# Attention inside a transformer block: products in blocks of two key tiles, reciprocals spread differently, the normalising product moved to GpSimd

## The chip, the cores and the metric

One core of a Trainium2 chip runs the whole program in one launch. The metric is device time in microseconds (us). The engines are TensorE (PE in the profile; its weight loads are PEld), VectorE (DVE), ScalarE (ACT), GpSimd (POOL) and SyncE (SP), whose queue issues the transfers.

## The reference

```python
def attn(x, qkv_w, qkv_b, proj_w, proj_b):     # 4 x 2048 tokens, 512 wide, 16 heads of 32
    q, k, v = split(x @ qkv_w.T + qkv_b)
    a = softmax(q @ k.T * 32 ** -0.5)          # per batch and head: 2048 x 2048
    return (a @ v) @ proj_w.T + proj_b
def ffn(x, Wr, br, W1, b1, W2, b2):            # 8 experts; each batch takes its top two by token 0
    h = gelu(x @ W1[idx] + b1[idx])
    return sum(h @ W2[idx] + b2[idx]) / 2
xn = layernorm(x)
out = x + attn(xn, ...) + ffn(xn, ...)
```

Everything is float32.

## The kernel before

There are three stages, one after the other. A dense stage makes queries, keys, values and the expert part; the attention stage (`attention_stage`, line 576) computes the softmax products; an output stage (`output_stage`, line 999) applies the last projection. Only the attention stage is changed.

**Groups and steps.** Four heads are handled together. A group is four heads by 512 queries; there are 64 groups (`NQ * QC`), in turns of `G = 8`, the first and last turn written out and six in a loop between them. Within a group the 2048 keys are 16 tiles of 128 (`KT`), and these are worked off in eight steps j = 0 to 7 (`NP`), two key tiles each.

**What TensorE does.** Its order is written out by hand in `STEPS`, one string a step, one letter a piece of work:

- S, a score product (`scores`, line 951): 128 keys by 512 queries of one head, into one of three banks `st_ps`. ScalarE takes the exponential of it into `p_sb` (line 814). A bank is used again when its exponential is done. 64 a group.
- U, a unit (`unit`, line 890): 128 queries by 512 keys of one head of a *coming* group, into one of three banks `mx_ps`. VectorE takes the largest value of each row (line 829); they become the shift of that group's softmax. Unit n waits until VectorE has reduced unit n - 3. 64 a group.
- V, the products of one key tile (`values`, line 902): four matmuls, one a head, 32 columns of the array each, over 512 queries. They need the key tile's four exponentials.
- Z, sum parts (`sums`, line 910): the same form with ones, over pairs of `p_sb` that GpSimd has added up (lines 756 and 766). `PARTS` says how many parts a Z holds: one in j = 0, 1, 4 and 6, two in j = 7.
- T, the transposition of the row maxima (line 895), once a group, in j = 6; it needs `max_done` of VectorE, and ScalarE makes the shift of it (line 780).

Before the change a step has two V, so a group has 16 places where TensorE goes from U and S to column-wise products and back, four pairs of U and S apart in the main.

**What the other engines do.** After the last product and the last sum part of a group, ScalarE copies `o_ps` to `o_raw` (`copy_o`, line 786, before its fourth exponential of the next group) and `sum_ps` to `sum_raw` (`copy_sum`, line 792). VectorE takes the reciprocals in eight pieces of 64 columns (`invert`, line 843), two in each of j = 2 to 5, and multiplies `o_raw` by them at the start of j = 6 (`normalise`, line 849). SyncE then stores `o_inv` (`store_group`, line 696), queued behind the load of the next shift and ahead of the next queries. GpSimd's order is `ADDS`, ten additions a group of 128 x 2048; the last one, of pair 7, has index 9 and waits for the group's last exponential.

```python
SB = 3
ADDS = [(0, 0, -1), (1, 1, -3), ("four", 1, None), (2, 0, None), (3, 2, -2), ("four", 2, None),
        (4, 0, None), (5, 1, 0), (6, 2, 1), (7, 0, 2)]
```

Of the kernel before, what the change touches and what calls it, by code (L numbers as in the profile page):

```python
# [18 lines left out]
ALU = mybir.AluOpType  # L19
# [14 lines left out]
NQ = B * HQ  # L34
KT = N // P
# [540 lines left out]
def attention_stage(nc, qh_d, ql_d, kh_d, kl_d, v_d, o_d):  # L576
# [6 lines left out]
    QC = N // TOK  # L583
    UN = 4 * TT * (N // 512)
    NP = KT // 2
    INV = 8
    SLOTS = 8
    AHEAD = 6
# [7 lines left out]
    PARTS = [(3, 1, 4), (6, 2, 6), (7, 0, 7), (8, 1, 7), (9, 2, 8), (10, 0, 9)]  # L596
    PAIR_ADDED = [[pair for pair, _, _ in ADDS].index(i) + 1 for i in range(NP)]
    NA, NS = len(ADDS), len(PARTS)
    ctx = ExitStack()
    with ctx:  # L600
        def sb(name, shape, dt):
# [2 lines left out]
        def sem(name):  # L604
# [12 lines left out]
        o_raw = sb("o_raw", [P, TOK], F32)  # L617
        sum_raw = sb("sum_raw", [P, TOK], F32)
        o_inv = sb("o_inv", [P, TOK], F32)
# [13 lines left out]
        exp_done, o_copied, sum_copied, shift_done = sem("exp_done"), sem("o_copied"), sem("sum_copied"), sem("shift_done")  # L633
# [3 lines left out]
        G = 2 * QC  # L637
# [4 lines left out]

        STEPS = ["USUSUSVZUSUSUSUSVUS", "USUSUSVZUSUSUSUSVUS", "USUSUSVUSUSUSUSVUS", "USUSUSVUSUSUSUSVUS",
                 "USUSUSVZUUSUSUSUSVUS", "USUSUSVUUSUSUSUSVUS", "SSSVZTSUSUSUSUVSUU", "USUSUSVZUSUSUSUSVUS"]
        FIRST = sum(s.count("U") for s in STEPS[AHEAD:])

        def unit_at(j, i):
# [7 lines left out]
        def bank(g, m):  # L657
            return (g * SK + m) % SB

        def bank_read(g, m):  # L660

            if m >= SB or g > 0:
                return g * SK + m - SB + 1
            return [n for n in range(-SB, 0) if bank(G, n) == bank(0, m)][0] + 1

        assert units_of(AHEAD - 1)[-1] == UN - 1 and "".join(STEPS).count("U") == UN
        assert all(step.count("S") == 8 for step in STEPS)

        with nc.Block() as block:
# [66 lines left out]
            @block.gpsimd  # L736
            def _(pool):
                pool.memset(ident[:, :], 0.0).then_inc(zeroed, 1)
                pool.wait_ge(zeroed, 1)
                pool.affine_select(out=ident[:, :], in_=ident[:, :], compare_op=ALU.not_equal, fill=1.0, base=0,  # L740
                                   pattern=[[-1, P]], channel_multiplier=1).then_inc(ident_ok, 1)

                pool.wait_ge(ident_ok, 1)
                pool.memset(ones[:, :], 1.0).then_inc(ones_ok, 1)
                for i in range(2):
                    pool.wait_ge(ones_ok, i + 1)
                    pool.memset(k_x[i][R:R + 1, :, :].bitcast(F32), 1.0).then_inc(ones_ok, 1)
                pool.wait_ge(ones_ok, 3)

                def turn(L):  # L750
                    for g in range(G):
                        for n, (i, slot, part) in enumerate(ADDS):
                            done = L * G * NA + g * NA + n
                            if i == "four":
                                pool.wait_ge(pair_done, done)
                                pool.tensor_tensor(p_pair[:, slot, :, :], p_pair[:, 0, :, :], p_pair[:, slot, :, :],  # L756
                                                   ALU.add).then_inc(pair_done, 1)
                                continue

                            pool.wait_ge(exp_done, L * G * SK + g * SK + 8 * i + 8)  # L760
                            if part is None:
                                pool.wait_ge(pair_done, done)
                            else:

                                pool.wait_ge(sum_done, since(L * G * NS, g * NS + part + 1))
                            pool.tensor_tensor(p_pair[:, slot, :, :], p_sb[:, 2 * i % SLOTS, :, :], p_sb[:, (2 * i + 1) % SLOTS, :, :],  # L766
                                               ALU.add).then_inc(pair_done, 1)

                turn(0)
                with pool.Fori(1, TURNS) as L:  # L770
                    turn(L)

            @block.scalar
            def _(act):
# [49 lines left out]
            @block.vector  # L824
            def _(dve):
                def unit(base, n):

                    dve.wait_ge(unit_ready, base + n + 1)
                    dve.reduce_max(unit_max[:, n // 4, n % 4:n % 4 + 1], mx_ps[n % 3][:, :], AX.X).then_inc(unit_done, 1)  # L829

                def rows(base, count):

                    dve.wait_ge(unit_done, base + UN)
                    dve.wait_ge(rows_ready, count - 1)
                    dve.reduce_max(row_max[:, :], unit_max[:, :, :], AX.X).then_inc(max_done, 1)

                def invert(count, part):

                    cols = slice(part * TOK // INV, (part + 1) * TOK // INV)
                    if part == 0:  # L840
                        dve.wait_ge(sum_copied, count)
                        dve.wait_ge(o_st, (count - 1) * 16)
                    dve.reciprocal(o_inv[:, cols], sum_raw[:, cols]).then_inc(inv_done, 1)  # L843

                def normalise(count):

                    dve.wait_ge(inv_done, count * INV)
                    dve.wait_ge(o_copied, count)
                    dve.tensor_tensor(o_inv[:, :], o_raw[:, :], o_inv[:, :], ALU.mult).then_inc(o_done, 1)

                for n in range(UN):
                    unit(0, n)
                rows(0, 1)
                for n in range(FIRST):
                    if n == 0:
                        dve.wait_ge(max_done, 1)
                    unit(UN, n)

                def turn(L, first, last):
                    for g in range(G):  # L860
                        for j in range(NP):
                            ahead = 2 if j >= AHEAD else 1
                            if j == AHEAD and not (first and g == 0):
                                normalise(L * G + g)
                            for i, n in enumerate(units_of(j)):
                                if not (last and g + ahead >= G):
                                    if n == 0:
                                        dve.wait_ge(max_done, L * G + g + 2)
                                    unit((L * G + g + ahead) * UN, n)
                                if 2 <= j < 6 and i in (2, 6) and not (first and g == 0):  # L870
                                    invert(L * G + g, 2 * (j - 2) + (i == 6))
                            if j == AHEAD - 1 and not (last and g + ahead >= G):
                                rows((L * G + g + ahead) * UN, L * G + g + 2)

                turn(0, True, False)
                with dve.Fori(1, TURNS - 1) as L:
                    turn(L, False, False)
                turn(TURNS - 1, False, True)
                for part in range(INV):
                    invert(NQ * QC, part)  # L880
                normalise(NQ * QC)

            @block.tensor
            def _(pe):
# [41 lines left out]
                def turn(L, first, last):  # L926
                    for g in range(G):
# [23 lines left out]
                            pe.matmul(st_ps[bank(g, m)][:, :], k_x[u][:, h, kt * P:(kt + 1) * P], q_x[qc][:, h, :],  # L951
                                      start=True, stop=True).then_inc(st_ready, 1)

                        def products(kt):

                            if kt < 0:
                                if not (first and g == 0):
                                    values(L, (g - 1) * KT + KT - 1, (g - 1) % G // QC, KT - 1)
                                return
                            if kt == 0:  # L960
                                pe.wait_ge(v_ld[u], (L + 1) * 16)
                                if not (first and g == 0):
                                    pe.wait_ge(o_copied, L * G + g)
                            values(L, g * KT + kt, u, kt)

                        def sum_parts(j):

# [8 lines left out]
                        for j in range(NP):  # L976
                            for i, step in enumerate(STEPS[j]):
                                if step == "U":
                                    next_unit(j, unit_at(j, i))
                                elif step == "S":  # L980
                                    scores(8 * j + STEPS[j][:i].count("S"))
                                elif step == "V":
                                    products(2 * j - 1 + STEPS[j][:i].count("V"))
                                elif step == "Z":
                                    sum_parts(j)
                                elif not (last and g == G - 1):
                                    turn_rows(L * G + g + 2)
# [2 lines left out]
                with pe.Fori(1, TURNS - 1) as L:  # L990
                    turn(L, False, False)
                turn(TURNS - 1, False, True)
                values(TURNS - 1, G * KT - 1, 1, KT - 1)
                for i in range(NS):
                    if PARTS[i][2] >= NP:
                        sums(TURNS - 1, G - 1, i)
# [181 lines left out]
```

## Time and profile before

| | |
|---|---|
| time, median of 3 runs | 5173.42 us (5172.55 to 5173.84) |
| the profiled execution's own time | 5168.91 us |
| its span in the trace | 5167.1 us |
| busy: PE, PEld | 97%, 56% of the span |
| busy: DVE, ACT, POOL | 66%, 50%, 63% of the span |
| attention stage | from about 1371 to 4975 us |

Busy shares are means over the three stages. In the timeline view, a row merges neighbouring instructions of one kind: the first number is the start, the second the length in us, x the count, and the bracket the idle time before it with what ended it. Matmuls are pipelined, so a row's length runs into the next row, and it is the distance from start to start that tells what a matmul costs.

### The profile page before, as it was taken

The numbers are of one execution on the slowest core, as the hardware profiler recorded it, in microseconds if no ns is written. First come the engines' busy times: TensorE is split into PE (matmuls) and PEld (weight loads), VectorE is DVE, ScalarE is ACT, GpSimd is POOL, SyncE is SP. The second block draws the span as 40 slices with busy tenths as digits, with TensorE's granted clock in tenths as the row PEclk, the third lists the DMA queues.
The fourth block names the chain that finished last, engine by engine and source line by source line (L and its number), as shares of the span: only waits on it lengthen the run. The fifth ranks groups of instructions, "written<-read, shape, count | busy, mean of one in ns | idle before, by whom it ended". The sixth has DMA issues, their size and how long they took to land. (4 is left out here: it accounts for less than half of the span.)

```text
span 5167.1 us, 83198 instructions
## 1 busy us (share of the span) xinstructions
PE 5031.4 (97%) x25932; PEld 2893.7 (56%) x25932; DVE 3420.5 (66%) x5616; ACT 2592.6 (50%) x4717; POOL 3231.8 (63%) x861
## 2 busy tenths in 40 slices
PE   8999999999899999999999999999999999999979
PEld 6878878788444444444444444444444444444447
DVE  4232232322678888877887887888788788888724
ACT  2121121211266666666666666666666666666631
POOL 1212111121488888887887888788788788888830
PEclk9999999999799999999999999999999999999989
DMA  5253343533402021121202102120220202020046
GB/s 171 88 158 95 117 130 97 153 94 106 102 20 53 17 52 42 32 53 24 50 19 56 48 22 53 24 50 20 57 50 20 56 18 50 20 56 17 7 164 238
DMA packets 186069, 348.49 MB, mean 67 GB/s; under 512 B 17956, under 2 KB 51748, under 8 KB 177448
## 3 DMA queue, kind: packets, MB, share of 16 engines
q1 hardware_dynamic: 185640, 342.99, 23.8%
q8 instruction: 242, 3.96, 0.3%
q14 instruction: 187, 1.53, 0.1%
HBM read 208.19 MB, written 134.22 MB: 66 GB/s over the span
## 5 line engine op out<-in xcount | busy, mean ns | idle before, releaser
L829 DVE TENSOR_REDUCE unit_max<-mx_ps 128x1 f32<-128x512 f32 x4096 | 2547.3, 682 | 664.0 <-PE mx_ps L890 617.8
L766 POOL TENSOR_TENSOR p_pair<-p_sb 128x2048 f32<-128x2048 f32 x512 | 2365.4, 4636 | 664.3 <-PE sum_ps L910 334.1
L814 ACT ACTIVATE p_sb<-st_ps 128x512 f32<-128x512 f32 x4096 | 2217.5, 599 | 1109.0 <-PE st_ps L951 1094.5
L890 PE MATMUL mx_ps<-k_x,q_x 96*128 96x512 f32 x4096 | 1734.9, 437 | 35.9 <-DMA k_x<-k_lo_d 19.6
L951 PE MATMUL st_ps<-q_x,k_x 97*128 97x512 f32 x4096 | 1621.1, 402 | 18.1 <-ACT p_sb L814 18.1
L890 PEld LDWEIGHTS mx_ps<-k_x,q_x 96*128 96x128 f32 x4096 | 771.6, 191 | 1042.5 <-DVE unit_max L829 787.6
L902 PE MATMUL o_ps<-p_sb,v_sb 128*32 128x512 f32 x8192 | 1093.8, 606 | 0.7 <-ACT p_sb L814 0.7
L951 PEld LDWEIGHTS st_ps<-q_x,k_x 97*128 97x128 f32 x4096 | 777.8, 190 | 239.2 <-ACT p_sb L814 120.1
L285 POOL TENSOR_TENSOR h_lo<-h_f,h_hi 128x512 fp32r<-128x512 f32 x128 | 165.0, 1290 | 689.1 <-DVE h_hi L469 689.1
L756 POOL TENSOR_TENSOR p_pair<-p_pair 128x2048 f32<-128x2048 f32 x128 | 587.5, 4590 | 10.0
L469 DVE CAST h_hi<-h_f 128x512 fp32r<-128x512 f32 x128 | 55.0, 431 | 540.7 <-ACT h_f L342 540.7
L342 ACT ACTIVATE h_f<-rot,b_sb 128x512 f32<-128x512 f32 x128 | 88.2, 689 | 643.5 <-PE rot L505 643.5
L910 PE MATMUL sum_ps<-p_pair,ones 128*32 128x512 f32 x3072 | 390.5, 595 | 7.0 <-POOL p_pair L766 4.7
L902 PEld LDWEIGHTS o_ps<-p_sb,v_sb 128*32 128x32 f32 x8192 | 161.4, 108 | 365.6 <-ACT p_sb L814 302.8
L843 DVE RECIPROCAL o_inv<-sum_raw 128x64 f32<-128x64 f32 x512 | 276.1, 541 | 64.2 <-ACT sum_raw L792 64.2
L326 ACT ACTIVATE qk_hi<-rot,qk_bias 128x512 fp32r<-128x512 f32 x128 | 88.2, 689 | 380.9 <-DMA q_lo_d<-qk_lo 161.4
L910 PEld LDWEIGHTS sum_ps<-p_pair,ones 128*32 128x32 f32 x3072 | 100.0, 111 | 240.2 <-issue 230.3
L503 PE MATMUL rot<-xnT_hi,wq_hi 128*128 128x512 f32 x512 | 202.0, 395 | 19.7 <-DVE qk_lo L433 10.8
L503 PE MATMUL acc<-we_hi,h_hi 128*128 128x512 f32 x512 | 205.3, 401 | 7.4 <-POOL h_lo L285 5.7
L433 DVE SCALAR_TENSOR_TENSOR qk_lo<-rot,qk_bias,qk_hi 128x512 fp32r<-128x512 f32 x128 | 95.8, 749 | 163.6 <-ACT qk_hi L326 163.4
L504 PE MATMUL rot<-xnT_lo,wq_hi 128*128 128x512 f32 x512 | 201.2, 393 | 0.0
L503 PE MATMUL rot<-xnT_hi,we_hi 128*128 128x512 f32 x512 | 199.6, 390 | 1.6 <-DVE v_out L455 1.6
(92 smaller groups left out, 3708.4 us busy)
## 6 DMA issues: line engine op xcount, KB each, us to landing
q_x<-q_hi_d SPq DMA_DIRECT2D x128, 256.0 KB, 5.3
k_x<-k_hi_d SPq DMA_DIRECT2D x30, 1024.0 KB, 9.8
xt<-x SPq DMA_DIRECT2D x64, 256.0 KB, 2.7
stage<-w SPq DMA_DIRECT2D x32, 512.0 KB, 5.1
q_hi_d<-qk_hi SPq DMA_DIRECT2D x64, 256.0 KB, 3.0
q_lo_d<-qk_lo SPq DMA_DIRECT2D x64, 256.0 KB, 3.8
k_hi_d<-qk_hi SPq DMA_DIRECT2D x64, 256.0 KB, 2.6
k_lo_d<-qk_lo SPq DMA_DIRECT2D x64, 256.0 KB, 3.3
```

Of the source, the lines that this page charges most:

```text
L285: pool.tensor_tensor(h_lo[:, n % 2, :], h_f[:, n % 2, :], h_hi[:, n % 2, :].bitcast(F32), ALU.subtract).then_inc(h_lo_done, 1)
L503: pe.matmul(out, lh, rh, start=start and k == 0, stop=False)
L504: pe.matmul(out, lh, rl, start=False, stop=False)
L756: pool.tensor_tensor(p_pair[:, slot, :, :], p_pair[:, 0, :, :], p_pair[:, slot, :, :], ALU.add).then_inc(pair_done, 1)
L766: pool.tensor_tensor(p_pair[:, slot, :, :], p_sb[:, 2 * i % SLOTS, :, :], p_sb[:, (2 * i + 1) % SLOTS, :, :], ALU.add).then_inc(pair_done, 1)
L814: act.activation(p_sb[:, kt % SLOTS, h, :], st_ps[bank(g, m)][:, :], ACT.Exp, scale=SCALE).then_inc(exp_done, 1)
L829: dve.reduce_max(unit_max[:, n // 4, n % 4:n % 4 + 1], mx_ps[n % 3][:, :], AX.X).then_inc(unit_done, 1)
L843: dve.reciprocal(o_inv[:, cols], sum_raw[:, cols]).then_inc(inv_done, 1)
L890: pe.matmul(mx_ps[n % 3][:, :], q_x[qc][0:R, h, t * P:(t + 1) * P], k_x[u][0:R, h, kc * 512:(kc + 1) * 512], start=True, stop=True).then_i ...
L902: op = pe.matmul(o_ps[rows, :], v_sb[u][:, kt, rows], p_sb[:, kt % SLOTS, h, :], start=(kt == 0), stop=(kt == KT - 1))
L910: op = pe.matmul(sum_ps[h * D:(h + 1) * D, :], ones[:, :], p_pair[:, slot, h, :], start=(i == 0), stop=(i == NS - 1))
L951: pe.matmul(st_ps[bank(g, m)][:, :], k_x[u][:, h, kt * P:(kt + 1) * P], q_x[qc][:, h, :], start=True, stop=True).then_inc(st_ready, 1)
```

## The change

A step now has one V, at the place of its first, and this V holds two key tiles: those of the step before (`products(j)`: tiles 2j - 2 and 2j - 1; in j = 0 the last two of the group before). The U and S that stood on both sides of the second V follow each other directly. The reciprocals of VectorE are handed out by a table `INVERT`, behind the last unit in front of a step's V: one piece in j = 2, one in j = 3, two in j = 4, three at the start of j = 6 and one in j = 7. The product with the reciprocals is taken from VectorE and given to GpSimd, ahead of its last addition of the group (`NORM = 9`), and after the last group behind everything else.

```diff
+    NORM = 9
-        STEPS = ["USUSUSVZUSUSUSUSVUS", "USUSUSVZUSUSUSUSVUS", "USUSUSVUSUSUSUSVUS", "USUSUSVUSUSUSUSVUS",
-                 "USUSUSVZUUSUSUSUSVUS", "USUSUSVUUSUSUSUSVUS", "SSSVZTSUSUSUSUVSUU", "USUSUSVZUSUSUSUSVUS"]
+        STEPS = ["USUSUSVZUSUSUSUSUS", "USUSUSVZUSUSUSUSUS", "USUSUSVUSUSUSUSUS", "USUSUSVUSUSUSUSUS",
+                 "USUSUSVZUUSUSUSUSUS", "USUSUSVUUSUSUSUSUS", "SSSVZTSUSUSUSUSUU", "USUSUSVZUSUSUSUSUS"]
+        INVERT = [(0, 0), (0, 0), (0, 1), (1, 2), (2, 4), (4, 4), (4, 7), (7, 8)]
...
+                def normalise(count):                      # GpSimd
+                    pool.wait_ge(inv_done, count * INV)
+                    pool.wait_ge(o_copied, count)
+                    pool.tensor_tensor(o_inv[:, :], o_raw[:, :], o_inv[:, :], ALU.mult).then_inc(o_done, 1)
...
+                            if n == NORM and not (first and g == 0):
+                                normalise(L * G + g)
...
-                def normalise(count):                      # VectorE
-                    dve.wait_ge(inv_done, count * INV)
-                    dve.wait_ge(o_copied, count)
-                    dve.tensor_tensor(o_inv[:, :], o_raw[:, :], o_inv[:, :], ALU.mult).then_inc(o_done, 1)
...
                             if j == AHEAD and not (first and g == 0):
-                                normalise(L * G + g)
+                                for part in range(*INVERT[j]):
+                                    invert(L * G + g, part)
...
-                                if 2 <= j < 6 and i in (2, 6) and not (first and g == 0):
-                                    invert(L * G + g, 2 * (j - 2) + (i == 6))
+                                if j != AHEAD and i + 1 == STEPS[j][:STEPS[j].index("V")].count("U") and not (first and g == 0):
+                                    for part in range(*INVERT[j]):
+                                        invert(L * G + g, part)
...
-                        def products(kt):
+                        def products(j):
...
+                            for kt in (2 * j - 2, 2 * j - 1):
+                                values(L, g * KT + kt, u, kt)
...
-                values(TURNS - 1, G * KT - 1, 1, KT - 1)
+                for kt in (KT - 2, KT - 1):
+                    values(TURNS - 1, (G - 1) * KT + kt, 1, kt)
```

## Rows read from the trace of the kernel before

**Rows 1.** Busy time by engine from 2000 to 4800 us (steady attention).

```profile
core 0: us, PE busy (x) PEld busy (x) DVE busy (x) ACT busy (x) POOL busy (x), PEclk, DMA share, GB/s
2000.00:4800.00 2800.00, 2773.16 (x15228) 1325.21 (x15230) 2282.69 (x3696) 1806.22 (x3345) 2304.69 (x500) 1.00 0.16 38
```

**Rows 2.** Waits from 2000 to 4800 us: total, times, longest.

```profile
PEld mx_ps L890 <- DVE unit_max L829: 606.3, 905, 0.8
...
PEld sum_ps L910 <- POOL p_pair L766: 1.3, 2, 0.7
```

**Rows 3.** Timeline of PE: four pairs, a V, and a V with a Z.

```profile
3000.51 0.50 PE L890 MATMUL mx_ps<-k_x,q_x 96*128 96x512 f32 x1
3000.85 0.40 PE L951 MATMUL st_ps<-q_x,k_x 97*128 97x512 f32 x1
...
3002.26 0.39 PE L951 MATMUL st_ps<-q_x,k_x 97*128 97x512 f32 x1
3002.58 1.07 PE L902 MATMUL o_ps<-p_sb,v_sb 128*32 128x512 f32 x8
3003.58 0.50 PE L890 MATMUL mx_ps<-k_x,q_x 96*128 96x512 f32 x1
...
3005.64 1.06 PE L902 MATMUL o_ps<-p_sb,v_sb 128*32 128x512 f32 x8
3006.52 1.04 PE L910 MATMUL sum_ps<-p_pair,ones 128*32 128x512 f32 x8
3007.49 0.50 PE L890 MATMUL mx_ps<-k_x,q_x 96*128 96x512 f32 x1
```

**Rows 4.** Timeline of PE: first U (or T) behind later blocks of the group.

```profile
3014.47 0.50 PE L890 MATMUL mx_ps<-k_x,q_x 96*128 96x512 f32 x1
...
3020.59 0.50 PE L890 MATMUL mx_ps<-k_x,q_x 96*128 96x512 f32 x1
...
3033.67 0.72 PE L890 MATMUL mx_ps<-k_x,q_x 96*128 96x512 f32 x2
...
3040.25 0.73 PE L890 MATMUL mx_ps<-k_x,q_x 96*128 96x512 f32 x2
...
3047.51 0.28 PE L895 MATMUL mx_ps<-ident_b,row_max 128*16 128x128 f32 x1
...
3056.10 0.50 PE L890 MATMUL mx_ps<-k_x,q_x 96*128 96x512 f32 x1
```

**Rows 5.** Timeline of PE: five units in a row, j = 4.

```profile
3034.95 0.50 PE L890 MATMUL mx_ps<-k_x,q_x 96*128 96x512 f32 x1
3035.28 0.40 PE L951 MATMUL st_ps<-q_x,k_x 97*128 97x512 f32 x1
3035.55 0.50 PE L890 MATMUL mx_ps<-k_x,q_x 96*128 96x512 f32 x1
...
3036.20 1.07 PE L902 MATMUL o_ps<-p_sb,v_sb 128*32 128x512 f32 x8
```

**Rows 6.** Timeline of DVE, the reductions behind two blocks.

```profile
3001.05 2.48 DVE L829 TENSOR_REDUCE unit_max<-mx_ps 128x1 f32<-128x512 f32 x4 [2.18 <-PE mx_ps L890]
...
3034.20 2.48 DVE L829 TENSOR_REDUCE unit_max<-mx_ps 128x1 f32<-128x512 f32 x4 [0.96 <-PE mx_ps L890]
```

**Rows 7.** Timeline of all engines, the exponentials behind a block.

```profile
3001.28 2.18 ACT L814 ACTIVATE p_sb<-st_ps 128x512 f32<-128x512 f32 x4 [2.78 <-PE st_ps L951]
```

**Rows 8.** Timeline of POOL: pair 7, then pairs 4 to 6 of the next group.

```profile
3005.10 4.59 POOL L766 TENSOR_TENSOR p_pair<-p_sb 128x2048 f32<-128x2048 f32 x1 [4.23 <-ACT p_sb L814]
...
3042.41 14.10 POOL L766 TENSOR_TENSOR p_pair<-p_sb 128x2048 f32<-128x2048 f32 x3
```

**Rows 9.** Lines 849 and 285 alone: shortest, median, longest ns.

```profile
L849 DVE TENSOR_TENSOR o_inv<-o_raw,o_inv x64: 692/2189/2403, 1476.7 to 4968.8; 128x512 f32<-128x512 f32 x64
```

```profile
L285 POOL TENSOR_TENSOR h_lo<-h_f,h_hi x128: 1262/1290/1298, 65.1 to 1307.5; 128x512 fp32r<-128x512 f32 x128
```

**Rows 10.** Timeline of PE at the loop's edge, and of POOL in the last group.

```profile
3173.55 0.50 PE L890 MATMUL mx_ps<-k_x,q_x 96*128 96x512 f32 x1 [2.21 <-issue]
```

```profile
4958.23 4.51 POOL L766 TENSOR_TENSOR p_pair<-p_sb 128x2048 f32<-128x2048 f32 x1 [0.44 <-ACT p_sb L814]
```

More of the change, by code:

```diff
@@ L748, in _, with turn @@
                 pool.wait_ge(ones_ok, 3)
-                def turn(L):
+                def normalise(count):
+                    pool.wait_ge(inv_done, count * INV)
+                    pool.wait_ge(o_copied, count)
+                    pool.tensor_tensor(o_inv[:, :], o_raw[:, :], o_inv[:, :], ALU.mult).then_inc(o_done, 1)
+                def turn(L, first):
                     for g in range(G):
@@ L767, in turn @@
                                                ALU.add).then_inc(pair_done, 1)
-                turn(0)
+                turn(0, True)
                 with pool.Fori(1, TURNS) as L:
-                    turn(L)
+                    turn(L, False)
+                normalise(NQ * QC)
             @block.scalar
@@ L880, in _ @@
                     invert(NQ * QC, part)
-                normalise(NQ * QC)
             @block.tensor
@@ L952, in scores @@
                                       start=True, stop=True).then_inc(st_ready, 1)
-                        def products(kt):
-                            if kt < 0:
+                        def products(j):
+                            if j == 0:
                                 if not (first and g == 0):
-                                    values(L, (g - 1) * KT + KT - 1, (g - 1) % G // QC, KT - 1)
+                                    for kt in (KT - 2, KT - 1):
+                                        values(L, (g - 1) * KT + kt, (g - 1) % G // QC, kt)
                                 return
-                            if kt == 0:
+                            if j == 1:
                                 pe.wait_ge(v_ld[u], (L + 1) * 16)
@@ L963, in products @@
                                     pe.wait_ge(o_copied, L * G + g)
-                            values(L, g * KT + kt, u, kt)
+                            for kt in (2 * j - 2, 2 * j - 1):
+                                values(L, g * KT + kt, u, kt)
                         def sum_parts(j):
@@ L982, in turn @@
                                 elif step == "V":
-                                    products(2 * j - 1 + STEPS[j][:i].count("V"))
+                                    products(j)
                                 elif step == "Z":
@@ L992, in _ @@
                 turn(TURNS - 1, False, True)
-                values(TURNS - 1, G * KT - 1, 1, KT - 1)
+                for kt in (KT - 2, KT - 1):
+                    values(TURNS - 1, (G - 1) * KT + kt, 1, kt)
                 for i in range(NS):
```

## The prediction

> **What bounds the kernel now.** I first read the windows view of the attention stage. TensorE shows 2773 of 2800 us busy, at the full granted clock; DVE has 2283, POOL 2305, ACT 1806 [rows 1]. So the order on TensorE sets the time, but busy time of pipelined matmuls doesn't say whether they run at their own pace. The waits answer this in part: 905 weight loads of units waited for a reduction of VectorE [rows 2]. In the timeline most of these lie under a V block and cost nothing; some don't. The reader should see two things there, the price of a V block and the pace of VectorE.
>
> **The price of a V block.** Between U and S the distance is 0.235 us (six of them from 3000.85 to 3002.26), behind a block the first is 0.34. Four pairs and a V come back to the same point after 3003.58 - 3000.51 = 3.07 us [rows 3]. The four pairs alone would be 8 x 0.235 = 1.88, so a V that stands alone costs 1.19. A column-wise piece directly behind a V comes only 0.88 after it (3005.64 to 3006.52), and a last piece of a block takes 0.97 to 1.00 until the next U [rows 3]. Joining two V therefore saves 1.19 - 0.88 = 0.31 us of TensorE, as long as nothing else holds it. Eight joins a group: 2.5 us of about 56. I take 0.88 for V behind V from Z behind V, the nearest row; its bounds are 0.88 and 1.00 (no overlap at all between them).
>
> The Trainium skill, page TensorEngine Tiling (Array Packing), Key Properties, says that a change of tiling mode drains TensorE. The rows agree that a block costs something at its edges. By that rule alone half of the drains go and the kernel becomes faster; this is the first rival.
>
> **The pace of VectorE.** Four reductions take 2.48 us from the first start to the last end [rows 6]. One is 0.69 long, so they start (2.48 - 0.69) / 3 = 0.60 us apart, while TensorE issues a unit every 0.47. The first starts 0.54 behind its unit (3000.51, 3001.05) [rows 3, 6]. With three banks, unit n needs reduction n - 3. The j = 4 stretch, five units in a row, shows what this does: the reductions start at 3034.20, 3034.80 and so on; the first ends at 3034.89 and the fourth unit comes at 3034.95, the fifth 0.60 later at 3035.55 [rows 5, 6]. So a held unit comes 0.69 + 0.06 = 0.75 behind the start of reduction n - 3, the next S 0.33 behind it, and a V that follows that S 0.65 behind the unit [rows 5].
>
> **A joined step, by these numbers.** Set the first U behind a block at 0. Reductions start at 0.54, 1.14, 1.74, 2.33, 2.93. U4 may come at 1.29 and U5 at 1.89, which holds up nothing. U6 comes at 1.74 + 0.75 = 2.49, when 2.46 was due, but with its weights loaded late, so that its S comes at 2.82 and not 2.69. U7 comes at 3.08, U8 at 3.68, and V at 3.68 + 0.65 = 4.33. Unheld, V would have come at 0.34 + 14 x 0.235 + 0.32 = 3.95. The run of eight pairs is thus paced by VectorE from the sixth unit on and loses 0.38, more than the join saves. Before the change the V after four pairs let VectorE catch up, in both halves of a step.
>
> The scores are no tighter: exponentials start (2.18 - 0.60) / 3 = 0.53 apart, the first 0.77 behind the U [rows 7, 3], and S7 needs the end of the fourth, at 2.96, when it is due beyond 3.0.
>
> **The sum over a group**, from block to block, before [rows 3, 4] and after:
> - stretches that end with V and Z (j = 0, 1, 4): 6.98 (3000.51 to 3007.49); after 4.33 + 0.88 + 0.88 + 0.97 = 7.06. Three of them: +0.24.
> - stretches that end with V only (j = 2, 3): 6.12 (3014.47 to 3020.59); after 4.33 + 0.88 + 1.00 = 6.21. Together +0.18.
> - j = 4 into 5, nine units in a row: 6.58 (3033.67 to 3040.25). U9 comes at 0.54 + 5 x 0.60 + 0.75 = 4.28, V at 4.93, the end at 6.81: +0.23.
> - j = 5 into 6, six units, then only S: 7.26 (3040.25 to 3047.51). The last S are held by exponentials; S7 at about 3.3, S8 at 3.9, V at 4.33, T at 7.06: -0.20. Here a V is saved and VectorE isn't in the way.
> - j = 6 into 7, nine units, three of them together: 8.59 (3047.51 to 3056.10). The first reduction starts 0.79 behind T, U9 comes at 0.79 + 5 x 0.60 + 0.75 = 4.53, V at 5.18, and V, V, Z, Z take 3.61: 8.79, +0.20.
>
> That is +0.65 us a group on 55.59. With 61 whole groups, +39.7. At each of seven edges between turns TensorE stands for 2.2 us [rows 10], in which VectorE catches up; that step gains 0.31 where I booked a loss of 0.08, so -2.7.
>
> **The reciprocals.** They stay 8 x 0.54 us, and each set now stands behind the unit in front of a V. VectorE ends the eighth reduction at 0.54 + 7 x 0.60 + 0.69 = 5.43, and its next unit is ready at 6.21 + 0.54 = 6.75. One piece fits in this 1.3 us; so do the two of j = 4, whose block has a Z (0.88 more). The three of j = 6 start behind the row maxima, near 4.6 in that stretch, and end near 6.2, with the next unit due at 7.06 + 0.79. Cost nothing, gain nothing: before, too, the pieces had gaps. Were this cover gone, each would hold up one unit by up to 0.54.
>
> **The product.** On VectorE it took 2.19 us [rows 9] at the start of j = 6, with idle time behind it, so its removal gives nothing. On GpSimd I take 1.29 us, the 128 x 512 subtraction of line 285 [rows 9]; a quarter of a pair's addition, 1.15 [rows 8], is the lower bound and 2.4, the longest on VectorE, the upper. It stands between pair 6 and pair 7. Pair 6 ends at 3042.41 + 14.10 = 3056.51, and POOL then waits 4.2 us for the exponentials of pair 7 [rows 8]. After the change these come some 1.1 us earlier, since no V lies before them; 3.1 us remain to hide 1.3, and up to 2.4. The last reciprocal is done before the V of j = 7, at about 3053, so the new wait on `inv_done` holds nothing. Behind POOL's wait is the addition of pair 7, for which only the last sum part, in j = 1, waits, and in the steady stage TensorE waited for POOL two times, 1.3 us in all [rows 2]. The store is issued some 9 us later; behind it in SP's queue is the load of queries, which waits for the next group's first scores anyway. `copy_o` of the next group needs `o_done` some 5 us after it is given. In the last group there are no units and POOL is the chain: pair 7 had waited only 0.44 [rows 10], so the product delays it by 0.85, and the final product is 1.29 and not 0.69 [rows 9]: +1.4.
>
> **Sum.** 39.7 - 2.7 + 1.4 = +38.4 us, or 0.7%. The profiled execution took 5168.9, which gives 5207; the median of the runs is 4.5 higher, 5173.4, which gives 5212. The measurement tells 0.2%, some 10 us, from no change.
>
> **Rivals.**
> - *The join pays and the held units don't show* (faster). The mechanism: an S whose bank is free starts its load while the U ahead of it waits, so that the late reduction holds only the unit. Then 0.31 x 8 x 62 = 154 less: 5020, or in part up to 5160. Against it: in j = 4 the S behind a held unit came 0.33 behind it, never before [rows 5]. It decides if a held U delays the V by under 0.3 us in place of 0.38. Chance 0.10.
> - The Trainium skill, page TensorE: Matmul & The Clock Gate, Part 3, The mechanism, tells of a 64-deep reorder window from which weight loads are pulled ahead of matmuls in flight. If that held past a waiting unit, this rival would be right; the trace of j = 4 shows no such thing.
> - *The two cancel* (within 0.2%): stall and saving differ by 0.07 in the plain steps, and if V behind V came 0.80 apart, or held S 0.27 behind their U, 0.65 a group would shrink to under 0.16. Time 5163 to 5184. Chance 0.14.
> - *V behind V doesn't overlap* (slower still): both V of a block at 1.00, +0.12 x 8 x 62 = 60 more: 5272. For it: the weights of each V are new, those of Z are always ones. Against it: Z behind V also changes weights. Chance 0.06.
> - *POOL comes late*: if its product were over 3.1 us, pair 7 would slip, and the sum part in j = 1 would catch it only after some 3 us more. Chance 0.02, 5220 to 5250.
>
> **Chances and range.** The forecast has 0.68, its own range 5190 to 5235. Slower by over 0.2%: 0.68 + 0.06 + 0.02 = 0.76; same 0.14; faster 0.10. The range reaches into the cancelling case below and halfway to the case without overlap above: 5172 to 5245.
>
> **What would show it.** The timeline of PE should have V, V 0.88 apart, then 1.00 to the next U; a plain step of 6.2 us; reductions of VectorE in rows of eight, 4.9 us long, 0.60 apart, with 1.3 idle behind them; the sixth to eighth unit of a run 0.60 apart and not 0.47; the waits of unit loads on VectorE fewer but uncovered; GpSimd's product near 1.3 us before pair 7 with an idle rest in front of pair 7. It is wrong if the units of a run keep 0.47, or if V behind V is far from 0.88.

## The result and the profile after

The changed kernel takes 5212.37 us (median of 4 runs, 5208.91 to 5214.97), the one before 5172.99 in the same comparison: a ratio of 1.0079, 95% interval 1.0067 to 1.0091. The forecast was 5212 us, slower. The profiled execution took 5214.17 us with a span of 5211.5, against 5168.91 and 5167.1 before.

Steady attention of the changed kernel in the windows view, to be held against [rows 1]:

```profile
2000.00:4800.00 2800.00, 2765.51 (x15046) 1290.35 (x15044) 2108.42 (x3598) 1763.70 (x3305) 2308.00 (x542) 0.99 0.16 38
```

TensorE is as busy as before and does 182 fewer matmuls in the same 2800 us (15046 against 15228). Its busy time alone would never show the loss. The waits of the same stretch do, against [rows 2]:

```profile
PEld mx_ps L899 <- DVE unit_max L843: 575.2, 1761, 0.8
```

The sum is even a little smaller, but 1761 loads of units waited in place of 905. Before, 605 of them were the first load behind a block and waited under a V block that ran anyway; now these are 149, and the new waits lie inside the runs. A plain step in the timeline of PE, from block to block:

```profile
3040.83 0.50 PE L899 MATMUL mx_ps<-k_x,q_x 96*128 96x512 f32 x1
3041.18 0.40 PE L960 MATMUL st_ps<-q_x,k_x 97*128 97x512 f32 x1
...
3042.82 0.41 PE L899 MATMUL mx_ps<-k_x,q_x 96*128 96x512 f32 x1
3043.06 0.40 PE L960 MATMUL st_ps<-q_x,k_x 97*128 97x512 f32 x1
3043.32 0.50 PE L899 MATMUL mx_ps<-k_x,q_x 96*128 96x512 f32 x1
...
3043.91 0.50 PE L899 MATMUL mx_ps<-k_x,q_x 96*128 96x512 f32 x1
...
3044.51 0.50 PE L899 MATMUL mx_ps<-k_x,q_x 96*128 96x512 f32 x1
...
3045.18 1.92 PE L911 MATMUL o_ps<-p_sb,v_sb 128*32 128x512 f32 x16
3047.03 0.50 PE L899 MATMUL mx_ps<-k_x,q_x 96*128 96x512 f32 x1
```

The fifth unit still comes on its beat. The sixth, seventh and eighth come at 2.49, 3.08 and 3.68 behind the first, 0.60 apart, and V at 4.35. Two V take 1.85 together. The step is 6.20 us, where two runs of four took 6.12 [rows 4]. VectorE in the same stretch:

```profile
3041.37 4.87 DVE L843 TENSOR_REDUCE unit_max<-mx_ps 128x1 f32<-128x512 f32 x8 [0.87 <-PE mx_ps L899]
3046.17 0.54 DVE L857 RECIPROCAL o_inv<-sum_raw 128x64 f32<-128x64 f32 x1
3047.57 4.87 DVE L843 TENSOR_REDUCE unit_max<-mx_ps 128x1 f32<-128x512 f32 x8 [0.86 <-PE mx_ps L899]
```

Eight reductions stand wall to wall, (4.87 - 0.69) / 7 = 0.60 apart. The reciprocal fits behind them, and 0.86 us of idle time are left in front of the next unit: VectorE isn't full, it is only full while the units come. GpSimd, against [rows 8]:

```profile
3006.42 13.65 POOL L779 TENSOR_TENSOR p_pair<-p_sb 128x2048 f32<-128x2048 f32 x3
3020.02 1.30 POOL L759 TENSOR_TENSOR o_inv<-o_raw,o_inv 128x512 f32<-128x512 f32 x1
3024.13 4.58 POOL L779 TENSOR_TENSOR p_pair<-p_sb 128x2048 f32<-128x2048 f32 x1 [2.81 <-ACT p_sb L828]
```

The product takes 1.30 us and 2.8 us of waiting for exponentials are left behind it. From T to T (the transposition, once a group) the group is now 56.15 us:

```profile
L904 PE MATMUL mx_ps<-ident_b,row_max x7: 277/278/278, 2843.3 to 3180.2; 128*16 128x128 f32 x7
```

(336.9 us for six groups.) The same view of the kernel before has 55.70, (3159.0 - 2824.8) / 6:

```profile
L895 PE MATMUL mx_ps<-ident_b,row_max x7: 276/277/278, 2824.8 to 3159.0; 128*16 128x128 f32 x7
```

That is 0.45 a group, about 27 us over the stage. The span has grown by 44.4. The rest shows at the edges between turns, where TensorE goes back to the head of the loop. Timeline of PE, the edge that answers to the one of [rows 10] (`issue` means that nothing the profile shows released the engine):

```profile
3190.91 0.41 PE L899 MATMUL mx_ps<-k_x,q_x 96*128 96x512 f32 x1
3191.16 0.39 PE L960 MATMUL st_ps<-q_x,k_x 97*128 97x512 f32 x1
3196.08 0.79 PE L899 MATMUL mx_ps<-k_x,q_x 96*128 96x512 f32 x1 [4.54 <-issue]
3196.67 0.63 PE L960 MATMUL st_ps<-q_x,k_x 97*128 97x512 f32 x1
3197.09 0.63 PE L899 MATMUL mx_ps<-k_x,q_x 96*128 96x512 f32 x1
```

TensorE stands for 4.54 us, not 2.21, and afterwards its matmuls come 0.42 apart and not 0.235: it runs at the lower of its two levels, 1.2 GHz. The windows view has the granted clock in the column behind the engines, first for 6 us behind the stand, then for the next 6, and last for the 5 us behind the stand of [rows 10] in the kernel before:

```profile
3196.00:3202.00 6.00, 5.92 (x30) 2.58 (x30) 2.08 (x3) 2.16 (x4) 1.03 (x1) 0.65 0.02 5
3202.00:3208.00 6.00, 6.00 (x36) 3.18 (x36) 4.88 (x8) 4.48 (x9) 0.00 (x0) 1.00 0.93 195
```

```profile
3173.50:3178.50 5.00, 4.95 (x22) 1.95 (x22) 1.98 (x3) 2.37 (x4) 3.17 (x1) 0.66 0.04 10
```

So the low clock is not new: it stood behind three of the edges before and stands behind all five now, mostly for longer. There are five such edges in either kernel, one at each jump back of the loop; where the loop is entered and left there is no such stand. Their gaps were 1.95, 2.27, 2.21, 1.93 and 1.94 us and are 3.42, 4.46, 4.54, 3.27 and 4.50. From T to T, the five groups that hold an edge are longer than plain ones by 19.2 us in sum before and by 31.7 after: 12.5 us of loss, 9.9 of them the gaps themselves. What is left of the 44.4 lies outside the groups: the first T comes 3.0 us later (nothing was changed in front of it, and among traces with whole reductions it lies between 1369 and 1377 us), the stretch behind the last T is 2.9 longer, the output stage 1.2 shorter.

### The profile page after: what moved, and what is told of

It reads as the page before. It is cut to its first block and busy times, and to the rows that moved or that the text cites. A ratio compares the mean times of both kernels' runs of the same rounds, so it can differ in the third digit from the quotient of the medians.

```text
span 5211.5 us, 83212 instructions
## 1 busy us (share of the span) xinstructions
PE 5069.7 (97%) x25932; PEld 2871.3 (55%) x25932; DVE 3235.3 (62%) x5552; ACT 2577.4 (49%) x4717; POOL 3279.8 (63%) x925
## 5 line engine op out<-in xcount | busy, mean ns | idle before, releaser
L843 DVE TENSOR_REDUCE unit_max<-mx_ps 128x1 f32<-128x512 f32 x4096 | 2496.8, 682 | 887.6 <-PE mx_ps L899 887.5
L779 POOL TENSOR_TENSOR p_pair<-p_sb 128x2048 f32<-128x2048 f32 x512 | 2335.2, 4582 | 659.6 <-PE sum_ps L919 419.3
L899 PE MATMUL mx_ps<-k_x,q_x 96*128 96x512 f32 x4096 | 1854.8, 461 | 53.1 <-DMA k_x<-k_lo_d 20.7
L911 PE MATMUL o_ps<-p_sb,v_sb 128*32 128x512 f32 x8192 | 991.2, 602 | 0.0
L911 PEld LDWEIGHTS o_ps<-p_sb,v_sb 128*32 128x32 f32 x8192 | 214.3, 109 | 490.6 <-ACT p_sb L828 251.2
L857 DVE RECIPROCAL o_inv<-sum_raw 128x64 f32<-128x64 f32 x512 | 251.2, 523 | 67.0 <-ACT sum_raw L806 67.0
L505 PE MATMUL acc<-we_hi,h_lo 128*128 128x512 f32 x512 | 201.2, 393 | 0.0
L505 PE MATMUL rot<-xnT_hi,wq_lo 128*128 128x512 f32 x512 | 201.1, 393 | 0.0
```

The source lines that it names most:

```text
L505: op = pe.matmul(out, ll, rh, start=False, stop=stop and k == len(pairs) - 1)
L899: pe.matmul(mx_ps[n % 3][:, :], q_x[qc][0:R, h, t * P:(t + 1) * P], k_x[u][0:R, h, kc * 512:(kc + 1) * 512], start=True, stop=True).then_i ...
L911: op = pe.matmul(o_ps[rows, :], v_sb[u][:, kt, rows], p_sb[:, kt % SLOTS, h, :], start=(kt == 0), stop=(kt == KT - 1))
```

## The experiments

Group lengths are from T to T inside a turn, read as above.

**Is it VectorE's pace? Two kernels with shorter reductions.** The same edit to both kernels; each reduction leaves out half of the columns:

```diff
-    dve.reduce_max(unit_max[:, n // 4, n % 4:n % 4 + 1], mx_ps[n % 3][:, :], AX.X)
+    dve.reduce_max(unit_max[:, n // 4, n % 4:n % 4 + 1], mx_ps[n % 3][:, 0:256], AX.X)
-    act.activation(p_sb[...], st_ps[...][:, :], ACT.Exp, scale=SCALE)
+    act.activation(p_sb[...], st_ps[...][:, :], ACT.Exp, scale=SCALE * 0.25)
```

> The kernel before, but each reduction of a unit looks at 256 of its 512 columns and the exponentials are scaled by a quarter more (so the softmax is another one; the instructions of all other engines are the same). A reduction then takes about 0.42 us and they start about 0.33 apart in place of 0.60. Both theories: the kernel before loses only a little to VectorE (held units in j = 4 to 7, some 0.5 to 0.9 us a group of 55.7), so 5115 to 5145 us. It is the base for the same edit with joined products.

> The changed kernel with the same shortened reductions (256 of 512 columns, exponentials scaled by a quarter more). Theory, VectorE paces the run of eight units and takes back what joining saves: with the pace gone the joins pay their 0.31 us each, 8 a group, so 2.2 to 2.5 us a group under e1_half_before, some 52.3 to 52.9 a group, near 4980 to 5000 us in all. Rival, joining saves nothing because V behind V doesn't overlap and VectorE has no part in it: within 0.3 us a group of e1_half_before, 5110 to 5150 us.

Measured: 5097.36 us (ratio to before 0.9864, 0.9849 to 0.9879) and 4957.28 (0.9592, 0.9577 to 0.9606). The first fell 18 us below its range, the second 23; some 8 us of either lie ahead of the first group, where TensorE only makes units (first T at 1363 us and not at 1371), which I had left out, and some 5 us more are the level of this comparison, in which the kernel before took 5167.65. For the second, the range of the time was also too high for its own range of the group: 52.3 us a group gives about 4960. The joins are now worth 140 us. The groups, first without and then with joins:

```profile
L895 PE MATMUL mx_ps<-ident_b,row_max x8: 276/277/278, 2732.5 to 3115.3; 128*16 128x128 f32 x8
```

```profile
L904 PE MATMUL mx_ps<-ident_b,row_max x8: 277/277/278, 2676.7 to 3043.1; 128*16 128x128 f32 x8
```

That is 54.69 and 52.34, so 2.35 for eight joins, 0.29 each against the 0.31 of the prediction. (Hardly a unit inside a run still waits for VectorE: 51 and 100 times in 2800 us.) In the timeline of PE of the second one the eighth unit and the products stand where an unheld run has them (V 3.97 behind the first unit), and a plain step is 5.82:

```profile
3017.73 0.50 PE L899 MATMUL mx_ps<-k_x,q_x 96*128 96x512 f32 x1
...
3020.66 0.40 PE L899 MATMUL mx_ps<-k_x,q_x 96*128 96x512 f32 x1
3021.14 0.39 PE L899 MATMUL mx_ps<-k_x,q_x 96*128 96x512 f32 x1
3021.70 1.92 PE L911 MATMUL o_ps<-p_sb,v_sb 128*32 128x512 f32 x16
3023.55 0.51 PE L899 MATMUL mx_ps<-k_x,q_x 96*128 96x512 f32 x1
```

So the joins do what they are meant to do, and it is the pace of the reductions that takes it back. The rival without overlap is out: in every joined kernel V comes 0.88 behind V.

**The parts by themselves.** One kernel has only the joins (the `STEPS`, `products` and last `values` of the diff, with the reciprocals and the product of the kernel before); the other has everything but these.

```diff
 # joins only: VectorE as before
+  STEPS = ["USUSUSVZUSUSUSUSUS", ...]
   if 2 <= j < 6 and i in (2, 6) and not (first and g == 0):
       invert(L * G + g, 2 * (j - 2) + (i == 6))
 # all but the joins: GpSimd's product and INVERT, with
   STEPS = ["USUSUSVZUSUSUSUSVUS", ...]
```

> The joined products alone: reciprocals where they were (behind the third and seventh unit of j = 2 to 5) and the product on VectorE. Theory, the loss is that of the joins: the reciprocals now fall inside a run of eight units, where VectorE sets the pace; two in each of j = 2 to 5, of which one lies in the first five units and holds the last ones up by 0.46, the other behind the seventh unit by less. That would make it worse than the changed kernel, by 1.0 to 2.5 us a group: 5270 to 5370 us. Rival, the reciprocals are covered wherever they stand: the same as the changed kernel, 5205 to 5220.

> Everything but the joins: the steps of the kernel before with two V, the reciprocals by the new table and the product on GpSimd. Theory, these two parts cost nothing by themselves: within 0.2% of before, 5165 to 5183; what little there is comes from the last group (product on POOL, up to 1.4 us). The table puts three reciprocals in a row in j = 6 where the product stood and these fit. Rival, the product on GpSimd is what makes the change slower: 5195 to 5215.

Measured: 5293.94 us (1.0243, 1.0229 to 1.0257) and 5170.86 (1.0006, 0.9997 to 1.0015). Reciprocals and product cost nothing that shows in the old steps (at most 0.15%); the product on GpSimd isn't what makes the change slower. In the joined steps the place of the reciprocals is worth 1.2 us a group (57.37 against 56.15): three of the stretches between blocks are 0.40 longer each, while the one in which VectorE's product stands is 8.76 in both kernels. Timelines of VectorE and PE with the joins only:

```profile
3018.97 2.48 DVE L829 TENSOR_REDUCE unit_max<-mx_ps 128x1 f32<-128x512 f32 x4 [0.87 <-PE mx_ps L890]
3021.37 0.54 DVE L843 RECIPROCAL o_inv<-sum_raw 128x64 f32<-128x64 f32 x1
3021.82 2.42 DVE L829 TENSOR_REDUCE unit_max<-mx_ps 128x1 f32<-128x512 f32 x4
3024.16 0.55 DVE L843 RECIPROCAL o_inv<-sum_raw 128x64 f32<-128x64 f32 x1
```

```profile
3021.51 0.50 PE L890 MATMUL mx_ps<-k_x,q_x 96*128 96x512 f32 x1
3021.85 0.40 PE L951 MATMUL st_ps<-q_x,k_x 97*128 97x512 f32 x1
3022.51 0.50 PE L890 MATMUL mx_ps<-k_x,q_x 96*128 96x512 f32 x1 [0.26 <-DVE unit_max L829]
```

A reciprocal between the fourth and the fifth reduction pushes the fifth by 0.45, and the eighth unit, which needs it, comes 1.00 behind the seventh and not 0.60. The step is 6.60 (3018.43 to 3025.03). The second reciprocal stands behind the eighth reduction and costs nothing in this step.

**The edge between turns.** In the last step of a turn the second of the two key tiles gets a V of its own again, one pair ahead of the branch:

```diff
+  steps = STEPS[j]
+  if j == NP - 1 and g == G - 1 and not last:
+      steps = steps[:-2] + "V" + steps[-2:]      # key tile KT - 2; j = 0 of the next turn has KT - 1 only
```

> The changed kernel, but in the last step of each turn the second of the two key tiles is again a V of its own, one pair before the branch to the next turn, as before the change (seven places in all; the rest stays joined). In the changed kernel TensorE stands 3.3 to 4.5 us at five of the edges, before it 1.9 to 2.3, and the granted clock is low behind more of them. Theory: the V in front of the last pair lets TensorE's sequencer reach the branch while the array is still at work; with it the gap is 1.9 to 2.5 again and the time 8 to 13 us shorter, near 5200 us. Rival: the longer gap comes from the code's size and place or varies by itself; the gaps stay at 3.3 to 4.5 and the time within 4 us of 5212.

> The changed kernel once more, unaltered, as the base for e10_moved_split and for a second reading of the gaps at the edges of the turns. Theory, the longer gaps belong to the code's order: 3.3 to 4.5 us at all five again, time 5205 to 5216 us. Rival, they vary from execution to execution and some of the five are near 2.

Measured: 5204.70 us (1.0061, 1.0048 to 1.0075) with the split; the changed kernel again, in another comparison, 5212.98 (1.0084, 1.0070 to 1.0098). The times differ by 8 us, at the lower end of the forecast, with intervals that just overlap; the gaps tell more. With the split they are 2.27, 1.89, 2.21, 2.05 and 2.20 us, in the changed kernel again 4.55, 4.37, 3.40, 4.43 and 4.46, and the groups at the edges lose 17.9 us against 31.7. Timeline of PE with the split:

```profile
3187.61 1.07 PE L911 MATMUL o_ps<-p_sb,v_sb 128*32 128x512 f32 x8
3188.61 0.50 PE L899 MATMUL mx_ps<-k_x,q_x 96*128 96x512 f32 x1
3188.95 0.39 PE L960 MATMUL st_ps<-q_x,k_x 97*128 97x512 f32 x1
3191.55 0.49 PE L899 MATMUL mx_ps<-k_x,q_x 96*128 96x512 f32 x1 [2.21 <-issue]
```

The profile shows the sequencer at the branch too: `COMPARE_BRANCH` of PE's sequencer, by its line, in the kernel before, the changed kernel and the one with the split (length in ns, start in us):

```profile
L990 PEldq COMPARE_BRANCH  x1: 3661/3661/3661, 3169.7 to 3169.7; - x1
```

```profile
L1001 PEldq COMPARE_BRANCH  x1: 4849/4849/4849, 3191.0 to 3191.0; - x1
```

```profile
L1007 PEldq COMPARE_BRANCH  x1: 3697/3697/3697, 3187.7 to 3187.7; - x1
```

The gap is the part of the branch that the array's last matmuls don't cover. With a V in front of the last pair the branch begins 1.5 to 1.7 us before those matmuls end, without it 0.4 to 0.5, at all five edges of all kernels here. That is 1.1 of the 2.0 us by which the mean gap grew, and the first half of the theory is shown. The other half is the branch itself: 3.52 us on the mean before, 4.36 in the changed kernel and 4.56 in its second trace, 3.60 with the split. It varies from one execution to another of the same kernel (4.85 and 3.71 us at the third edge), and two kernels with a V in front of the last pair, e1_half_before and e7_unit_last_two, had branches of up to 4.7 and 5.1 us, so that their gaps were 1.8 to 3.2 and 2.1 to 3.9. What sets its length stays open, so the rival isn't out for this half.

**Putting the units elsewhere.** If the last units of a run come early only by the order of the letters, another order should mend it:

```diff
-  "USUSUSV..."      # the three pairs in front of a V, all steps but j = 6
+  "SUSUSUV..."
```

The kernel with two V a step has this swap in front of both V (the first `USUSUSVZUSUSUSUSVUS` becomes `SUSUSUVZUSSUSUSUVUS`), and not only in front of the first, as its expectation says.

> The changed kernel, but the three pairs in front of a V are S U in place of U S (in all steps but j = 6), so the last unit of a run stands directly in front of the products, and units 6 to 8 come 0.235 later when they are due. Theory, a held unit costs what it is late and no more: the eighth unit is due at 3.63 and VectorE lets it come at 3.68, so V follows near 4.05 and not at 4.33; a plain step 5.95 us, a group 54.4 to 54.6, the time 5105 to 5120 us, below both kernels. Rival, the run is bound by the sum of VectorE's and TensorE's work and the order inside it doesn't matter: 5205 to 5220.

> The kernel before (two V a step, reciprocals and product as before) with the same swap of the three pairs in front of the first V. It tells how much of e6_unit_last is the swap and how much the joins. Before, only j = 4, 5 and 7 had held units; the swap spares these, some 0.5 to 0.7 us a group: 5128 to 5145 us. If the joins pay once the units stand right, e6_unit_last is below this one by 15 to 40 us; if not, the two are equal.

Measured: 5119.94 us (0.9897, 0.9882 to 0.9913) with joins, 5148.71 (0.9949, 0.9935 to 0.9962) without. The groups are 54.76 and 55.23 us. Both are faster than either kernel. The first is at the upper end of its range, the second 4 us over it. A plain step with joins, timeline of PE:

```profile
3042.41 0.50 PE L905 MATMUL mx_ps<-k_x,q_x 96*128 96x512 f32 x1
...
3044.63 0.79 PE L966 MATMUL st_ps<-q_x,k_x 97*128 97x512 f32 x2
3045.26 0.39 PE L905 MATMUL mx_ps<-k_x,q_x 96*128 96x512 f32 x1
...
3045.75 0.39 PE L905 MATMUL mx_ps<-k_x,q_x 96*128 96x512 f32 x1
...
3046.25 0.39 PE L905 MATMUL mx_ps<-k_x,q_x 96*128 96x512 f32 x1
3046.57 1.92 PE L917 MATMUL o_ps<-p_sb,v_sb 128*32 128x512 f32 x16
3048.42 0.50 PE L905 MATMUL mx_ps<-k_x,q_x 96*128 96x512 f32 x1
```

V stands 4.16 behind the first unit and not 4.35, the step is 6.01 and not 6.20. The forecast of 5.95 took no wait of the scores into account; two scores now follow each other (x2 in the second row) and the waits on exponentials rose from 34.6 us (98 times) to 192.3 (793 times) in 2800. With the units placed so, the joins are worth 28.8 us.

**Units moved between steps as well**. One run of nine units is left (from j = 0 into 1) in place of two, and scores stand in pairs between the units:

```diff
+  STEPS = ["SSUSUVZUSUSSUSUSUU", "SSUUSUVZUSUSSUUSSU", "USSUSUVUSUSSUUSUS", "USSUSUVUSUSUSUSSUU",
+           "SSUSUVZUSUSUSUSS", "UUSSUSUVUSUSSUUSUSUU", "SSSVZTSUUSSUSUSU", "SUSUSUVZUSUSSUSUSUU"]
```

> The changed kernel with units moved between steps too, so that a run between two blocks has no more of them than VectorE reduces in it, and none is due earlier than 0.6 us behind the one before on the mean. By the same recurrence a group takes 53.8 to 53.9: 5065 to 5080 us. The rival is GpSimd: from its first addition, released by the sum part of j = 1, to the end of pair 5, which the parts of j = 7 need, it takes 37.3 us, about what TensorE then needs for the same stretch; if it is late the sum parts of j = 7 wait, and the time stays above 5085.

> Both corrections together: the units moved as in e8_unit_moved and the V taken apart again in the last step of a turn as in e5_edge_split. If the two terms are independent, it is 8 to 13 us below e8_unit_moved, 5068 to 5076 us, with gaps of 1.9 to 2.7 at the edges. Rival: behind the split V there are two units and no score, and the second unit waits for VectorE; if that holds the sequencer up, the gaps stay near 4 and the time at 5078 to 5086.

Measured: 5081.69 us (0.9821, 0.9808 to 0.9835), and with the split 5075.62 (0.9819, 0.9805 to 0.9832). The group is 54.10 in the first, whose time lies 2 us over its range; the second is within its own, but 4 of the 6 us between them are the level of the comparison (the kernel before took 5173.99 and 5169.64). GpSimd was not late: sum parts waited for it nine times in 2800 us, 2.7 us in all. The split shortened the gaps here too, from between 3.8 and 4.4 us to between 2.1 and 2.6, but the two ratios, from different comparisons, can't be told apart, so the 8 to 13 us that the split should give are not shown here. Either is 1.8% under the kernel before.

## Why the prediction was right, and where its terms were off

- **The price of a join.** 0.31 us each was forecast; with VectorE out of the way it is 0.29. V behind V takes 0.88 as assumed, and the way back to the next unit 0.97 (together the 1.85 above).
- **The pace of VectorE.** Sixth, seventh and eighth unit at 2.49, 3.08 and 3.68: forecast and measured alike; V at 4.35 for 4.33. The plain step is 6.20 for 6.21, the stretch with Z 7.05 for 7.06, nine units in j = 4 6.79 for 6.81, j = 5 into 6 7.04 for 7.06, j = 6 into 7 8.76 for 8.79. Shorter reductions turned the loss into a gain of 140 us, which is the mechanism shown and not only argued.
- **The group.** +0.65 was forecast and +0.45 came. Half of the miss is the sum of those hundredths; the other half is the length before: I took one group of 55.59, from first unit to first unit, and the mean of six is 55.70. Over the stage: 27 us in place of 39.7, so this term was 12.5 too high. This is a mis-sized term.
- **The edges.** Here a step of the prediction was wrong, not only its size. It said that at each of seven edges TensorE stands for 2.2 us, as before, that VectorE catches up in it and the join pays: -2.7 us. Only five edges have a stand, at the jumps back of the loop, and its length was no constant: the change moved a V away from in front of the branch, the stand grew to 3.3 to 4.5 us with more time at 1.2 GHz behind it, and the edges cost 12.5 us. This term was 15 us too low.
- **Luck in the total.** The two errors have opposite signs and nearly cancel; that the median was met to a microsecond is luck. The profiled executions show a growth of 45.3 us where 38.4 were forecast, the medians one of 39.4. Of the 6.9 us that the first is over, 2.7 are these two errors, and most of the rest lies in front of the first group and behind the last, in terms that the prediction put at nothing.
- **Reciprocals and product.** Cost nothing: 1.0006 for both in the old steps. The price of lost cover, up to 0.54 for a reciprocal in a run, was right as well: 0.40 a step with the joins alone. The product took 1.30 for 1.29. Behind it 2.8 us of waiting were left, not 1.8: the exponentials of pair 7 came only 0.1 us earlier behind pair 6 and not 1.1, which did no harm.
- **The tail.** In the last group GpSimd's product has no wait to hide in. From the last T to its end it is 1.5 us longer in this trace and 3.0 in the second one of the same kernel; 1.4 were forecast.
- **The rivals.** An S that slips past a waiting unit was not seen: S came 0.33 to 0.34 behind each held unit. The Trainium skill, page TensorE: Matmul & The Clock Gate, Part 3, The mechanism, tells of weight loads pulled ahead of matmuls in flight; the trace doesn't show this for a load that stands behind a waiting one. The drain at a change of tiling mode, which the Trainium skill, page TensorEngine Tiling (Array Packing), Key Properties, states, is in line with the 0.29 that a join saves, though no trace shows the drain itself. By that rule alone the change would have been faster, as it is once VectorE's pace is out of the way.

## What to carry to other kernels

Whether a saving on the engine that sets the time is kept depends on what the saved work was hiding: a block that looks like overhead may be the time in which a slower engine empties its few banks, though that engine is far from full on the mean. Take the run between two such pauses, write down when the k-th item may start by the slower engine's pace and the number of banks, and compare it with when it is due; here three banks, 0.60 and 0.47 us gave the step to 0.02. Then place the paced items as late in the run as they are due, and look separately at what stands in front of a loop's branch.

## What the runs showed of the hardware

- At the jump back of a loop whose body has eight groups, the branch of TensorE's sequencer took 3.3 to 5.1 us, and TensorE stood for 1.8 to 4.6 us of it. With a column-wise block in front of the last two pieces before the branch it was 1.9 to 2.6 in four kernels and up to 3.9 in two others; without it 3.3 to 4.6 in all. Behind the stands of 4.5 us in the changed kernel the clock stayed at 1.2 GHz, with matmuls 0.42 apart, for 4 to 7 us.
- A product of two 128 x 512 operands on VectorE waits for the addition that GpSimd has begun. In all four kernels that have it there it ended 0.55 us behind the end of that addition, in 252 of 252 cases, so its length in the profile is that of the wait: median 2.19 us before [rows 9], 3.05 in e1_half_before, 2.47 in e7_unit_last_two and 0.77 in e3_join_only; 0.69 where GpSimd was idle. GpSimd's own product took 1.25 to 1.34 wherever it stood.
- Four column-wise matmuls (a V: 32 columns of the array each, over 512 queries) come 0.88 us behind four others; a V that stands alone between full-width matmuls costs 1.19 [rows 3].
